# An edge-gated graph layer on one core: what GpSimd waits for between its trains of gathers

## The chip, the cores and the metric

The kernel runs on one core of a Trainium2 chip. The metric is the device time of one execution in microseconds (us). Engines are called as in the profile: PE (TensorE), DVE (VectorE), ACT (ScalarE), POOL (GpSimd), SP (SyncE).

## What is computed

A graph of 12500 nodes with 64 features and 412500 edges, sorted by target node, with 32 attributes each. Cut to what matters:

```python
h = relu(layernorm(x))                    # [12500, 64]
h0 = edge_attr @ W0 + b0                  # [412500, 64]
t = gelu(gelu(h0) @ W1 + b1) @ W2 + b2
score = (h0 + t) @ W3 + b3                # [412500, 64]
msg = h[src] * score                      # one gathered row for each edge
wV = segment_sum(msg, dst) / max(count, 1)
out = x + wV @ Wo + bo
```

## The kernel before

The edges are worked on in 403 blocks of 1024 (8 tiles of 128). For each block:

- **SP** loads the edge attributes twice (`pair`, `act_in`), four blocks ahead, and every eight blocks the source indices (`idx`).
- **POOL** issues eight indirect DMAs (L329), one for each tile: each fetches 128 rows of `h` by `src` into a slot of `rows`. There are 16 slots, one for each block of a ring of 16 (`G_RING`). Their landings count up a semaphore for each slot, `gathered[slot]`.
- **PE** does four things in this order for a step b: `second` (L437, `ps_h1`, of block b), `first` (L431, `ps_h0`, of block b + 1), `sums` (L455, `ps_w`, of block b - 1) and `last` (L446, `ps_s`, the score of block b). Each ends with one increment of a semaphore: `h1_done`, `h0_done`, `sums_done`, `score_done`.
- **ACT** takes the Gelu of `ps_h0` (L386) and of `ps_h1` (L391, two halves).
- **DVE** builds a one-hot matrix (L607), multiplies score by gathered rows into `msg` (L615, waits for `score_done` and `gathered`), and adds the window of sums into `acc` (L720, waits for `sums_done`).

`ps_s`, `ps_h1`, `ps_h0`, `ps_w` have two buffers each: names that end in a belong to even blocks, those in b to odd ones. After block 391 PE and DVE turn the finished part of `acc` into output (`project_early`, L484), and the last five blocks before it each carry a large DVE addition, L678. The gathers of the first 16 blocks are issued at the start, the first six from `x` itself before `h` is stored. Those of block b + 16 are issued in step b of POOL's loop, `gather_ahead`, after

```python
pool.wait_ge(msg_done, b + 1)                            # the slot is free again
if s % 2 == 0:
    pool.wait_ge(score_done, b + (G_RING - LAG + 1))     # LAG = 8
```

So at every second block POOL waits until PE has scored the block eight before the one whose rows it is about to gather, and then issues 16 gathers in a row.

Of the kernel before, what the change touches and what calls it, by code (L numbers as in the profile page):

```python
# [32 lines left out]
TILES = 8  # L33
# [15 lines left out]
G_RING = 16  # L49
IDX_GROUP = 8  # L50
IDX_GROUPS = 4
LAG = 8
IN_RING = 4
RAW = 6
LN_ROWS = 25
# [19 lines left out]
def edge_gated_layer(nc, x, edges, src, dst, dst_rows, weights, out):  # L75

    with ExitStack() as ctx:
# [6 lines left out]
        def sem(name):  # L84
            return ctx.enter_context(nc.semaphore(name))
# [83 lines left out]
        gathered = [sem(f"gathered{s}") for s in range(G_RING)]  # L169
# [4 lines left out]
        score_done = sem("score_done")  # L174
# [29 lines left out]
        def blocks_loop(eng, first, end, unroll, step):  # L204

            turns = (end - first) // unroll
            if turns < 2:
                turns = 0
            else:
                with eng.Fori(0, turns) as i:  # L210
                    for u in range(unroll):
                        step(i * unroll + (first + u), first + u)
            for b in range(first + turns * unroll, end):
                step(b, b)

        def uses(b, ring):

            return (b >> ring.bit_length() - 1) + 1

        def tiles_of(b):  # L220
            return LAST_TILES if isinstance(b, int) and b == NB - 1 else TILES
# [95 lines left out]
        @block.gpsimd  # L317
        def _(pool):
            pool.iota(iota_i[:, :], pattern=[[1, WIN]], base=0, channel_multiplier=0
                      ).then_inc(set_up, 1)  # L320

            def gather(b, s, table):
                slot, part, at = s % G_RING, s // IDX_GROUP % IDX_GROUPS, s % IDX_GROUP
                if at == 0:
                    pool.wait_ge(idx_in[part], uses(b, IDX_GROUP * IDX_GROUPS) * 16)

                pool.sem_inc(gathers_begun, 1)
                for t in range(tiles_of(b)):
                    pool.indirect_dma_start(  # L329
                        rows[:, slot, t, :], None, table,  # L330
                        bass.IndirectOffsetOnAxis(ap=idx[:, part, at, t:t + 1], axis=0),
                    ).then_inc(gathered[slot], 16)

            for b in range(RAW):
                gather(b, b, x)

            pool.wait_ge(h_out, 32 * LN_STEPS)
            for b in range(RAW, G_RING):
                if b == G_RING // 2:

                    pool.wait_ge(bounds_step, 1 + 2 * CHUNKS)
                    pool.sem_inc(gathers_begun, 1)
                gather(b, b, h_dram)

            def gather_ahead(b, s):

                pool.wait_ge(msg_done, b + 1)
                if s % 2 == 0:

                    pool.wait_ge(score_done, b + (G_RING - LAG + 1))  # L350
                gather(b + G_RING, s + G_RING, h_dram)

            blocks_loop(pool, 0, NB - G_RING, IDX_GROUP * IDX_GROUPS, gather_ahead)


# [490 lines left out]
```

## Time and profile before

| | |
|---|---|
| median of 3 runs | 4955.2 us (4943.95 to 4957.94) |
| the profiled execution: time | 4910.35 us |
| its span, first to last instruction | 4908.4 us |
| granted TensorE clock, mean | 0.999 of full speed (2.4 GHz) |
| busy share of the span | PE 77%, POOL 63%, ACT 20%, DVE 14% |
| gathers on POOL | 3175 of `h`, 3026.5 us busy, 953 ns each |
| DMA | 46 GB/s over the span |

A busy share is an average over the span. The profile's time of a gather on POOL is the making of its descriptors, not the arrival of its rows. "Idle before" is the time that an engine stood still before an instruction, and behind the arrow stands what ended it; "remote" stands where the profile finds no instruction of this core that ended just then, and "issue" where no wait is seen.

### The profile page before, as it was taken

The numbers are of one execution on the slowest core, as the hardware profiler recorded it, in microseconds if no ns is written. First come the engines' busy times: TensorE is split into PE (matmuls) and PEld (weight loads), VectorE is DVE, ScalarE is ACT, GpSimd is POOL, SyncE is SP. The second block draws the span as 40 slices with busy tenths as digits, with TensorE's granted clock in tenths as the row PEclk, the third lists the DMA queues.
The fourth block names the chain that finished last, engine by engine and source line by source line (L and its number), as shares of the span: only waits on it lengthen the run. The fifth ranks groups of instructions, "written<-read, shape, count | busy, mean of one in ns | idle before, by whom it ended". The sixth has DMA issues, their size and how long they took to land.

```text
span 4908.4 us, 44284 instructions
## 1 busy us (share of the span) xinstructions
PE 3760.6 (77%) x14718; PEld 2533.1 (52%) x14719; DVE 708.9 (14%) x1349; ACT 987.5 (20%) x1332; POOL 3082.5 (63%) x3228
## 2 busy tenths in 40 slices
PE   2487777777777777777777777777777777777788
PEld 1355555555555555555555555555555555555566
DVE  5011111111111111111111111111111111111122
ACT  3112112221122211221122211222112121121211
POOL 7366666666666666666666666666666666666661
PEclk9999999999999999999999999999999999999999
DMA  4111111111111111111111111111111111111111
GB/s 122 28 46 44 45 44 46 46 45 44 44 46 46 44 45 44 46 47 44 44 45 45 46 44 44 44 45 47 44 44 46 44 47 44 44 46 44 46 37 47
DMA packets 223796, 227.46 MB, mean 46 GB/s; under 512 B 118540, under 2 KB 118669, under 8 KB 223352
## 3 DMA queue, kind: packets, MB, share of 16 engines
q0 software_dynamic: 103136, 105.82, 9.9%
q1 hardware_dynamic: 119968, 117.76, 8.4%
q10 hardware_dynamic: 616, 3.20, 0.2%
q14 instruction: 68, 0.56, 0.0%
q8 instruction: 8, 0.13, 0.0%
HBM read 220.11 MB, written 6.40 MB: 46 GB/s over the span
## 4 chain that ended last, share of the span: by engine, by line
another core or an unknown queue 63%; PE 25%; DVE 4%; DVEq 3%; issue 3%; POOL 1%; ACT 0%; DMA 0%; ACTq 0%; POOLq 0%
PE ps_sb L446 14%; PE ps_wa L455 8%; DVE msg L615 3%; DVEq L715 2%; POOL rows L329 1%; DVEq L614 1%; PE ps_sa L446 1%; PE ps_h1a L437 0%; PE ps_h0a L431 0%; PE ps_h0b L431 0%; PE ps_wb L455 0%; PE ps_h1a L484 0%; PE ps_h1b L437 0%; DVE acc L720 0%
## 5 line engine op out<-in xcount | busy, mean ns | idle before, releaser
L329 POOL DMA_INDIRECT rows<-h_rows,idx x3175 | 3026.5, 953 | 1739.0 <-issue 1005.5
L455 PE MATMUL ps_wa<-ln_sq,msg 128*65 128x64 f32 x3230 | 407.2, 319 | 1035.2 <-DVE msg L615 1035.2
L455 PEld LDWEIGHTS ps_wa<-ln_sq,msg 128*65 128x65 f32 x3230 | 369.7, 229 | 1348.6 <-DVE msg L615 1335.1
L391 ACT ACTIVATE act_in<-ps_h1b,wp 64x512 f32<-64x512 f32 x402 | 275.0, 684 | 2446.5 <-remote 2377.6
L446 PE MATMUL ps_sa<-w_last,act_in 97*128 97x64 f32 x3232 | 729.9, 420 | 11.1 <-ACT act_in L391 9.2
L446 PE MATMUL ps_sb<-w_last,act_in 97*128 97x64 f32 x3216 | 728.1, 421 | 0.6 <-ACT act_in L391 0.6
L446 PEld LDWEIGHTS ps_sa<-w_last,act_in 97*128 97x128 f32 x3232 | 711.9, 332 | 13.0 <-ACT act_in L391 9.0
L446 PEld LDWEIGHTS ps_sb<-w_last,act_in 97*128 97x128 f32 x3216 | 710.4, 333 | 2.3 <-issue 1.5
L615 DVE TENSOR_TENSOR msg<-ps_sa,rows 128x512 f32<-128x512 f32 x202 | 139.7, 691 | 3034.6 <-remote 2973.3
L391 ACT ACTIVATE act_in<-ps_h1a,wp 64x512 f32<-64x512 f32 x404 | 276.4, 684 | 1308.7 <-PE ps_h1a L437 1019.2
L455 PEld LDWEIGHTS ps_wb<-ln_sq,msg 128*65 128x65 f32 x3216 | 368.1, 229 | 303.5 <-issue 302.9
L437 PE MATMUL ps_h1b<-g,wp 128*128 128x512 f32 x402 | 406.4, 1112 | 35.7 <-ACT g L386 29.9
L431 PE MATMUL ps_h0a<-pair,wp 64*128 64x512 f32 x404 | 418.5, 1137 | 1.9 <-issue 1.9
L437 PE MATMUL ps_h1a<-g,wp 128*128 128x512 f32 x404 | 408.3, 1114 | 15.1 <-ACT g L386 13.4
L431 PE MATMUL ps_h0b<-pair,wp 64*128 64x512 f32 x402 | 416.5, 1138 | 0.0
L455 PE MATMUL ps_wb<-ln_sq,msg 128*65 128x64 f32 x3216 | 405.6, 319 | 1.5 <-issue 1.5
L615 DVE TENSOR_TENSOR msg<-ps_sb,rows 128x512 f32<-128x512 f32 x201 | 139.0, 692 | 985.9 <-PE ps_sb L446 905.8
L607 DVE TENSOR_TENSOR ln_sq<-dst_i,iota 128x512 f32<-128x512 f32 x403 | 277.8, 690 | 8.4 <-issue 8.4
L431 PEld LDWEIGHTS ps_h0a<-pair,wp 64*128 64x128 f32 x404 | 101.2, 309 | 304.3 <-issue 304.2
L431 PEld LDWEIGHTS ps_h0b<-pair,wp 64*128 64x128 f32 x402 | 100.3, 310 | 302.4 <-issue 302.4
L386 ACT ACTIVATE g<-ps_h0b,wp 128x512 f32<-128x512 f32 x201 | 138.2, 687 | 89.9 <-PE ps_h0b L431 51.5
L386 ACT ACTIVATE g<-ps_h0a,wp 128x512 f32<-128x512 f32 x202 | 138.9, 688 | 12.4 <-PE ps_h0a L431 5.5
(63 smaller groups left out, 719.4 us busy)
## 6 DMA issues: line engine op xcount, KB each, us to landing
pair<-in_edges SPq DMA_DIRECT2D x403, 128.0 KB
act_in<-in_edges SPq DMA_DIRECT2D x403, 128.0 KB
rows<-h_rows,idx POOLq DMA_INDIRECT x3175
xs<-in_x SPq DMA_DIRECT2D x4, 700.0 KB
h_rows<-ln_d ACTq DMA_DIRECT2D x4, 700.0 KB
dst_i<-in_dst SPq DMA_DIRECT2D x1, 1612.0 KB
idx<-in_src SPq DMA_DIRECT2D x50, 32.0 KB
rows<-in_dst_rows SPq DMA_DIRECT2D x4, 384.0 KB
```

Source lines behind the costliest of these rows:

```text
L329: pool.indirect_dma_start(rows[:, slot, t, :], None, table, bass.IndirectOffsetOnAxis(ap=idx[:, part, at, t:t + 1], axis=0),).then_inc(gat ...
L386: act.activation(g1[:, s % 2, :], ps_h0[s % 2][:, :], ACT.Gelu, bias=b0).then_inc(g1_done, 1)
L391: act.activation(act_in[0:D, s % IN_RING, g, :], ps_h1[s % 2][g * D:(g + 1) * D, :], ACT.Gelu, bias=wp[g * D:(g + 1) * D, C_B1:C_B1 + 1]). ...
L431: pe.matmul(ps_h0[s % 2][:, :], w0, pair[:, s % IN_RING, :], start=True, stop=True).then_inc(h0_done, 1)
L437: pe.matmul(ps_h1[s % 2][:, :], w1, g1[:, s % 2, :], start=True, stop=True).then_inc(h1_done, 1)
L446: mm = pe.matmul(ps_s[s % 2][:, t * D:(t + 1) * D], act_in[:, s % IN_RING, g, j * P:(j + 1) * P], w_last[:, :], start=(t == 0), stop=(t == ...
L455: last = pe.matmul(window, msg[:, s % 2, t, :], onehot[:, t, :], start=(t == 0), stop=(t == n - 1))
L607: return dve.tensor_tensor(to, rel.unsqueeze(2).to_broadcast([P, TILES, WIN]), iota_tiles, ALU.is_equal)
L614: dve.wait_ge(gathered[s % G_RING], (uses(b, G_RING) - 1) * 16 * TILES + 16 * n)
L615: dve.tensor_tensor(msg[:, s % 2, 0:n, 0:D], ps_s[s % 2][:, 0:n * D].rearrange("p (t d) -> p t d", d=D), rows[:, s % G_RING, 0:n, :], ALU. ...
L715: base = dve.value_load(base_b[0:1, one(b)], min_val=0, max_val=N - 1)
```

## The change

In place of the score of eight blocks back, POOL waits at every second block for the landing of all gathers of the block before. The wait now stands in `gather` itself, so it also holds in the first 16 blocks; the wait for the free slot stays.

```diff
-LAG = 8
@@ def gather(b, s, table):
                 if at == 0:
                     pool.wait_ge(idx_in[part], uses(b, IDX_GROUP * IDX_GROUPS) * 16)
+                if s > 0 and s % 2 == 0:
+
+                    pool.wait_ge(gathered[(s - 1) % G_RING], uses(b - 1, G_RING) * 16 * TILES)
 
                 pool.sem_inc(gathers_begun, 1)
@@ def gather_ahead(b, s):
                 pool.wait_ge(msg_done, b + 1)
-                if s % 2 == 0:
-
-                    pool.wait_ge(score_done, b + (G_RING - LAG + 1))
                 gather(b + G_RING, s + G_RING, h_dram)
```

`uses(b, ring)` is b // ring + 1, the number of times that the slot has been used with block b.

## Rows read from the trace of the kernel before

**Rows 1.** The page: the chain that ended last, its shares by engine.

```profile
another core or an unknown queue 63%; PE 25%; DVE 4%; DVEq 3%; issue 3%; POOL 1%; ACT 0%; DMA 0%; ACTq 0%; POOLq 0%
```

**Rows 2.** Timeline, one train of gathers and its ends: start, duration, engine, instruction, idle before.

```profile
2001.15 2.02 PE L437 MATMUL ps_h1b<-g,wp 128*128 128x512 f32 x2
...
2005.52 0.94 POOL L329 DMA_INDIRECT rows<-h_rows,idx  x1 [0.30 <-issue]
...
2009.49 1.39 ACT L391 ACTIVATE act_in<-ps_h1b,wp 64x512 f32<-64x512 f32 x2 [12.78 <-remote]
2009.62 0.69 DVE L615 TENSOR_TENSOR msg<-ps_sa,rows 128x512 f32<-128x512 f32 x1 [13.98 <-remote]
...
2010.20 0.94 POOL L329 DMA_INDIRECT rows<-h_rows,idx  x1 [3.73 <-remote]
...
2010.37 2.02 PE L455 MATMUL ps_wa<-ln_sq,msg 128*65 128x64 f32 x16 [5.20 <-DVE msg L615]
...
2016.01 0.69 DVE L615 TENSOR_TENSOR msg<-ps_sb,rows 128x512 f32<-128x512 f32 x1 [4.64 <-PE ps_sb L446]
...
2028.95 0.95 POOL L329 DMA_INDIRECT rows<-h_rows,idx  x1 [0.30 <-issue]
```

**Rows 3.** Waits of the stretch 241 to 4698: who waited for whom, us, times, longest.

```profile
PE ps_wa L455 <- DVE msg L615: 960.2, 187, 5.7
...
POOL rows L329 <- remote: 666.5, 176, 4.1
```

**Rows 4.** Busy time by stretch: us, then PE, PEld, DVE, ACT, POOL, clock, DMA.

```profile
187.00:241.00 54.00, 52.09 (x213) 36.61 (x214) 9.40 (x19) 14.90 (x20) 0.00 (x0) 1.00 0.11 30
241.00:1241.00 1000.00, 786.59 (x3064) 525.71 (x3062) 130.82 (x258) 202.07 (x277) 645.22 (x680) 1.00 0.18 45
```

**Rows 5.** Groups by line, stretch 241 to 4698: the gathers.

```profile
L329 POOL DMA_INDIRECT rows<-h_rows,idx x3024 | 2872.0, 950 | 1644.2 <-issue 914.9 <-remote 666.5 <-PE ps_sa L446 62.8
```

**Rows 6.** Timeline of the start, blocks 1 to 8.

```profile
95.51 0.69 DVE L615 TENSOR_TENSOR msg<-ps_sb,rows 128x512 f32<-128x512 f32 x1 [3.67 <-remote]
...
107.55 1.39 ACT L391 ACTIVATE act_in<-ps_h1a,wp 64x512 f32<-64x512 f32 x2 [17.77 <-remote]
...
177.72 0.95 POOL L329 DMA_INDIRECT rows<-h_rows,idx  x1 [0.30 <-issue]
...
187.54 0.69 DVE L615 TENSOR_TENSOR msg<-ps_sa,rows 128x512 f32<-128x512 f32 x1 [82.23 <-remote]
...
240.72 0.69 DVE L615 TENSOR_TENSOR msg<-ps_sa,rows 128x512 f32<-128x512 f32 x1 [7.43 <-PE ps_sa L446]
...
241.45 0.95 POOL L329 DMA_INDIRECT rows<-h_rows,idx  x1 [62.78 <-PE ps_sa L446]
```

**Rows 7.** Timeline: the last gather of block 5, and DVE, which waits for its landing.

```profile
73.07 0.95 POOL L329 DMA_INDIRECT rows<-in_x,idx  x1 [0.30 <-issue]
...
75.46 1.22 DVE L580 TENSOR_REDUCE ln_sum<-rows 128x16 f32<-128x1024 f32 x1 [12.80 <-DMA rows<-in_x,idx]
```

**Rows 8.** Timeline of POOL, DVE and ACT in blocks 387 to 391, with L678.

```profile
4715.96 0.94 POOL L329 DMA_INDIRECT rows<-h_rows,idx  x1 [0.31 <-remote]
4717.21 2.80 POOL L329 DMA_INDIRECT rows<-h_rows,idx  x1 [0.30 <-issue]
...
4717.10 1.48 DVE L678 TENSOR_TENSOR xs<-xs,wp 120x1280 f32<-120x1280 f32 x1
...
4719.34 0.69 ACT L386 ACTIVATE g<-ps_h0a,wp 128x512 f32<-128x512 f32 x1 [2.12 <-remote]
...
4731.63 0.69 DVE L615 TENSOR_TENSOR msg<-ps_sa,rows 128x512 f32<-128x512 f32 x1 [5.52 <-PE ps_sa L446]
...
4740.81 0.69 DVE L615 TENSOR_TENSOR msg<-ps_sb,rows 128x512 f32<-128x512 f32 x1 [6.15 <-PE ps_sb L446]
```

**Rows 9.** Timeline: two scored blocks after the last gather.

```profile
4854.85 0.69 DVE L615 TENSOR_TENSOR msg<-ps_sb,rows 128x512 f32<-128x512 f32 x1 [7.55 <-PE ps_sb L446]
...
4864.03 0.69 DVE L615 TENSOR_TENSOR msg<-ps_sa,rows 128x512 f32<-128x512 f32 x1 [7.54 <-PE ps_sa L446]
```

## The prediction, on record before the changed kernel ran

> **What bounds the kernel now.** I read the page first. Its chain of what ended last gives 63% of the span to no instruction at all and only 25% to PE [rows 1], so the span is mostly a wait whose author the profile can't name. The timeline of one stretch shows the wait. PE ends the matmuls of ps_h1b at 2001.15 + 2.02 = 2003.17, yet ACT, which waits for nothing else, starts on them at 2009.49; DVE starts on ps_sa, finished before them, at 2009.62 [rows 2]. Both are released within 0.13 us of each other by "remote". PE's work was done; its signals came 6.3 us late. PE itself then waits 5.20 us for DVE's msg [rows 2], and this happens once for two blocks, 187 times, 960 us between 241 and 4698 [rows 3].
>
> When are the signals late? The reader should look at POOL beside them. In 187 to 241 POOL is idle and PE is busy 52.09 of 54 us; from 241 on POOL is busy 645 of 1000 us and PE 787 [rows 4]. After the last gather a block takes 4864.03 - 4854.85 = 9.18 us [rows 9]. In a train of 16 gathers, 2010.20 to 2028.95 + 0.95 = 2029.90 [rows 2], the signals of the first ten us come in time (msg of ps_sb at 2016.01) and those due later wait for the end of the train: 2009.49 is 3.03 us after the previous train's last gather (2005.52 + 0.94 = 2006.46) [rows 2]. At the start, where POOL issues gathers without a break until 178.67, blocks 1 and 2 are 187.54 - 95.51 = 92 us apart [rows 6]. So a long unbroken train of gathers holds back PE's signals, and a pause sets them free. I don't know the mechanism, only this law.
>
> The cycle before is therefore: a train of 19.70 us, then a pause that lasts until the held score arrives, since it is just this score that POOL waits for, 3.73 us [rows 2]; POOL's waits of this kind are 666.5 / 176 = 3.79 us [rows 3]. 19.70 + 3.79 = 23.5 us for two blocks. Checked against the whole: from block 8 (240.72) to block 391 (4740.81) it is 4500.1 / 383 = 11.75 us a block [rows 6, 8], 3024 / 16 = 189 trains [rows 5].
>
> **The change part by part.** *Removed:* the wait for the score. POOL's pause no longer depends on when PE's signals get through. *Added:* a wait for the landing of the previous block's last gather. Its price has one near row: the last gather of block 5 ends on POOL at 74.02, and DVE, which waited for its landing, starts at 75.46, 1.44 us later [rows 7]. POOL's own way from a released wait to its next gather is 2010.20 - 2009.49 = 0.71 us [rows 2]. Together a pause of 2.15 us in place of 3.79. The bounds: not below 1.7 (DVE's own start taken out of the 1.44 and the reaction overlapped), not above 2.6 (landing beside full traffic). I take 2.15. The cycle becomes 19.70 + 2.15 = 21.85 us, 10.93 a block.
>
> What is queued behind this wait on POOL is only the next gathers and their index wait. Who waits for them is DVE's msg, and the gathers run seven to eight blocks ahead, some 80 us, so nobody feels it directly. SP's index loads hang on msg_done, which freed them for four groups of eight blocks ahead; POOL reaches at most two groups ahead, so they stay in time. The wait for the free slot stays: POOL may now run up to 16 blocks ahead, but if PE does two blocks for each train it never gets there.
>
> Does PE do two blocks in 21.85 us? It needs 18.4 [rows 9]. If the held signals come 3.03 us after a train's last gather as now, that is 0.9 us after the new train's start; the next score, 6.5 us on (2016.01 after 2009.49, [rows 2]), lies at 7.4 us in the train, still in its free part; the one after at about 16.5 us, held until the next pause. Two scores a cycle, then, and POOL is the bound.
>
> The open question is whether a pause of 2.15 us frees them at all, because POOL resumes before the 3.03 us are over. The rows nearest to it are those of blocks 387 to 391. There DVE's long addition (1.48 us) stretches single gathers: that at 4717.21 takes 2.80 in place of 0.95, so POOL makes no headway for 1.85 us [rows 8]. ps_h0a, held until then, reaches ACT at 4719.34, 2.4 us after the previous gather's end at 4716.90, while POOL has not been given a longer break [rows 8]. With such an addition at every block and no real pause, msg follows msg after 4740.81 - 4731.63 = 9.18 us, PE's full speed [rows 8, 9]. A break of 1.85 us in the train thus does what the long one does. But these breaks come once a block, those of the change once in two blocks, after 20 us of gathers; that is why I am not sure.
>
> The page "GPSIMD Engine Reference" of the Trainium skill (section Specifications) says that POOL shares its interface to SBUF with DVE and contends with DVE instructions that have two SBUF inputs; by it these stretches are POOL at rest, not POOL at other work, and the trace agrees (2.80 us beside the two-input addition of 1.48 us). The page "DMA: Bandwidth & Descriptors" puts the fixed cost of a DMA at about 2.0 us, mostly the receipt of the write; as an estimate from it, a landing wait of 1.05 us behind the descriptors, a pause of 1.8 and a total some 65 us lower. No gather's landing is timed by itself in the rows, so I stay with the 2.15.
>
> **The sum**, against the profiled execution's 4910.35 us:
>
> - Blocks 8 to 391: 383 x (11.75 - 10.93) = -314 us.
> - Start, blocks 1 to 8: now 240.72 - 95.51 = 145 us, most of it the 82 us in which the signals were held [rows 6]. The new wait also breaks the trains there, at blocks 8, 10, 12 and 14, so 7 x 10.93 = 77 us: -68. Bounds 0 (the signals stay held as now) and -75; I take -60, for the first blocks' uneven start.
> - Early projection (project_early) and the last eleven blocks: POOL is still some seven blocks ahead and is done during the projection; unchanged, 0.
>
> Together 4910 - 314 - 60 = 4536 us. The median of the runs lies 45 us above the profiled execution (4955.2 against 4910.35); I carry this over: 4580 us, -7.6%. With the pause between 1.7 and 2.6 us and the start's bounds: 4490 to 4650.
>
> **The rivals.**
>
> 1. *The short pause frees nothing* (slower). The signals need 3 us of silence, POOL is back after 2.15. Then POOL runs on to the 16th slot and stops there for msg_done. For it: at the start signals were held for 82 us, and the first came 8.9 us after the last gather (187.54 against 178.67) [rows 6], so a deep jam isn't gone at once. Against it: rows 8. Its time: release 3.03 us after the train, msg 0.13 + 0.69, POOL 0.71, a pause of 4.6 us; 24.3 a cycle, +0.8 x 192 = +155, and +40 at the start, where PE no longer gets its free run of 187 to 241: about 5150 us, up to 5400 if a landing wait falls amid each train as well. Chance 0.20.
> 2. *Some pauses work, some don't.* Each miss costs PE about one cycle of 21.85 us that it can't regain while POOL stays two blocks a cycle. The gain of 374 us is used up by 17 misses among 192 trains; with 4 to 15 misses the time is 4650 to 4930. For it: the start of the present kernel, where single signals slip through at odd moments (107.55) [rows 6]. Chance 0.12.
> 3. *No change*, within 0.3%: POOL is faster and PE takes it up with waits elsewhere, or misses happen to balance: 4955. No row speaks for it; chance 0.04.
>
> My forecast has the remaining 0.64. The point that decides between it and rival 1 is one number: whether PE's signals arrive within about 3 us of a train's end although POOL restarts at 2.15.
>
> **Numbers.** 0.3% is about what a measurement here can tell from no change. Faster: 0.64 + 0.11 = 0.75; same 0.04; slower 0.21. The range reaches from 4480 over the partly working pauses and no change to 4990, which leaves out nearly only rival 1; the forecast's own range is 4490 to 4650.
>
> **What the changed profile would show.** If right: trains of 16 gathers with 2.1 to 2.2 us before every 17th; ACT and DVE released "remote" about 3 us after a train's last gather, with POOL already in its next; PE's wait before ps_w about 3.5 us in place of 5.2; no gap of 80 us at the start and none of 62.78 us on POOL; two blocks in 21.9 us. If rival 1 holds: POOL's pauses of 4 to 5 us ended just after DVE's msg, and a lead of 16 blocks. Rival 2 would show as PE waits of 20 us and more. The prediction fails if the pause is much longer than 2.6 us, or if the score due 7.4 us into a train is already held (then PE would do one block a train and rival 1 takes over).

## The result, and the profile after

The changed kernel takes 5181.21 us (median of 4 runs, 5179.42 to 5183.77), the kernel before 4955.07 us beside it: ratio 1.0469, 95% interval 1.0446 to 1.0491. It is 4.7% slower; the forecast was 7.6% faster. The profiled execution took 5179.42 us. Its page:

```profile
span 5177.4 us, 44320 instructions
...
PE 3753.1 (72%) x14718; PEld 2528.3 (49%) x14719; DVE 709.0 (14%) x1349; ACT 986.1 (19%) x1332; POOL 3096.5 (60%) x3228
...
PEclk9555555555555555555555555555555555555555
...
L331 POOL DMA_INDIRECT rows<-h_rows,idx x3175 | 3042.0, 958 | 1864.6 <-issue 1154.5
```

No engine has noticeably more work than before: the gathers are 3042.0 us in place of 3026.5, PE has 3753.1 in place of 3760.6, and no share is higher. Nearly all of the added time is waiting. The granted clock is 0.5 (1.2 GHz) from the second slice on, where before it was 2.4 GHz; that looks like a cause and isn't one (below). Line numbers have moved by one or two: POOL L331, DVE's msg L614, ACT L385 and L390, PE L430 to L454.

The waits of the changed kernel (who waited for whom, us in total, times, longest):

```profile
DVE msg L614 <- remote: 3293.0, 193, 83.1
...
PE ps_wa L454 <- DVE msg L614: 1210.9, 191, 8.9
...
POOL rows L331 <- DVE msg L614: 705.6, 144, 6.6
```

These sums are over the whole span. The second line has 191 waits and 1035.2 us in the trace before: PE now waits longer. The third is new: POOL waited for the held score itself [rows 3], and waits now for DVE's msg, which comes after it. The landing is not what ends its pauses. The timeline of one cycle (start, duration, idle before):

```profile
2001.57 0.94 POOL L331 DMA_INDIRECT rows<-h_rows,idx  x1 [0.30 <-issue]
...
2005.40 1.39 ACT L390 ACTIVATE act_in<-ps_h1b,wp 64x512 f32<-64x512 f32 x2 [14.02 <-remote]
2005.55 0.69 DVE L614 TENSOR_TENSOR msg<-ps_sa,rows 128x512 f32<-128x512 f32 x1 [16.33 <-remote]
...
2007.15 0.98 POOL L331 DMA_INDIRECT rows<-h_rows,idx  x1 [4.64 <-DVE msg L614]
...
2030.30 0.69 DVE L614 TENSOR_TENSOR msg<-ps_sa,rows 128x512 f32<-128x512 f32 x1 [16.61 <-remote]
...
2031.90 0.97 POOL L331 DMA_INDIRECT rows<-h_rows,idx  x1 [4.93 <-DVE msg L614]
```

The last gather ends at 2001.57 + 0.94 = 2002.51, the held signals reach ACT 2.89 us and DVE 3.04 us later, DVE multiplies for 0.69, and POOL is back 0.91 us after that: 4.64 us. Before, POOL was back 0.71 us after the score, beside DVE's multiplication [rows 2]. The cycle is now 2031.90 - 2007.15 = 24.75 us.

How did POOL come to be 16 blocks ahead? The start shows it:

```profile
135.12 0.94 POOL L331 DMA_INDIRECT rows<-h_rows,idx  x1 [2.35 <-issue]
136.10 0.69 DVE L614 TENSOR_TENSOR msg<-ps_sa,rows 128x512 f32<-128x512 f32 x1 [19.21 <-remote]
...
179.10 0.94 POOL L331 DMA_INDIRECT rows<-h_rows,idx  x1 [2.29 <-DMA rows<-h_rows,idx]
...
181.27 0.69 DVE L614 TENSOR_TENSOR msg<-ps_sb,rows 128x512 f32<-128x512 f32 x1 [43.41 <-remote]
...
201.13 0.94 POOL L331 DMA_INDIRECT rows<-h_rows,idx  x1 [2.30 <-issue]
...
223.13 0.94 POOL L331 DMA_INDIRECT rows<-h_rows,idx  x1 [2.33 <-issue]
...
245.00 0.94 POOL L331 DMA_INDIRECT rows<-h_rows,idx  x1 [2.22 <-DMA rows<-h_rows,idx]
...
266.13 0.69 DVE L614 TENSOR_TENSOR msg<-ps_sa,rows 128x512 f32<-128x512 f32 x1 [83.10 <-remote]
...
284.00 1.09 POOL L331 DMA_INDIRECT rows<-h_rows,idx  x1 [6.57 <-DVE msg L614]
290.12 0.69 DVE L614 TENSOR_TENSOR msg<-ps_sa,rows 128x512 f32<-128x512 f32 x1 [5.84 <-PE ps_sa L445]
```

Here the pauses are near the predicted ones, 2.22 to 2.35 us for a landing. Two of the six are followed soon by a held msg (136.10 and 181.27, 0.98 and 2.17 us after POOL is back); four are not (157.14, 201.13, 223.13, 245.00), and the last three of these fall into 83 us without a msg. At 284.00 the ring is full, since POOL has issued the gathers of blocks 0 to 22 and needs block 7's msg for the next, and the first pause ended by msg comes.

The 269.0 us between the spans (5177.4 - 4908.4) are then accounted for. Block 8 is reached at 290.12 in place of 240.72 [rows 6]: +49.4. From block 8 to 391, at 5020.81 in the trace after, it takes 4730.7 us in place of 4500.1: +230.6, or 12.35 us a block against 11.75. The rest is 156.6 against 167.6 us: -11.0. The medians lie only 226 us apart, because the profiled execution before was 45 us below the median of its kernel and the one after only 2 us below.

### The profile page after: what moved, and what is told of

Same layout as the page of the kernel before. It is cut to its first block, busy times and chain, and to the rows that moved or that the text cites. A ratio compares the mean times of both kernels' runs of the same rounds, so it can differ in the third digit from the quotient of the medians.

```text
span 5177.4 us, 44320 instructions
## 1 busy us (share of the span) xinstructions
PE 3753.1 (72%) x14718; PEld 2528.3 (49%) x14719; DVE 709.0 (14%) x1349; ACT 986.1 (19%) x1332; POOL 3096.5 (60%) x3228
## 4 chain that ended last, share of the span: by engine, by line
another core or an unknown queue 65%; PE 24%; DVE 4%; DVEq 3%; issue 2%; ACT 0%; POOL 0%; DMA 0%; ACTq 0%
PE ps_sb L445 13%; PE ps_wa L454 8%; DVE msg L614 3%; DVEq L714 2%; DVEq L613 1%; PE ps_sa L445 1%; PE ps_h1a L483 0%; PE ps_h1b L483 0%; PE ps_h1a L436 0%; PE ps_h0a L430 0%; PE ps_wb L454 0%; DVE acc L719 0%; PE ps_h1b L436 0%; PE ps_h0b L430 0%
## 5 line engine op out<-in xcount | busy, mean ns | idle before, releaser
L331 POOL DMA_INDIRECT rows<-h_rows,idx x3175 | 3042.0, 958 | 1864.6 <-issue 1154.5
L454 PE MATMUL ps_wa<-ln_sq,msg 128*65 128x64 f32 x3230 | 406.8, 319 | 1277.0 <-DVE msg L614 1210.9
L454 PEld LDWEIGHTS ps_wa<-ln_sq,msg 128*65 128x65 f32 x3230 | 369.4, 228 | 1590.3 <-DVE msg L614 1509.9
L390 ACT ACTIVATE act_in<-ps_h1b,wp 64x512 f32<-64x512 f32 x402 | 274.5, 683 | 2729.8 <-remote 2673.4
L614 DVE TENSOR_TENSOR msg<-ps_sa,rows 128x512 f32<-128x512 f32 x202 | 139.7, 692 | 3300.0 <-remote 3234.9
L454 PEld LDWEIGHTS ps_wb<-ln_sq,msg 128*65 128x65 f32 x3216 | 367.7, 228 | 334.0 <-issue 333.5
L390 ACT ACTIVATE act_in<-ps_h1a,wp 64x512 f32<-64x512 f32 x404 | 275.7, 683 | 1308.0 <-issue 994.4
L454 PE MATMUL ps_wb<-ln_sq,msg 128*65 128x64 f32 x3216 | 405.1, 319 | 32.8 <-issue 32.8
L430 PE MATMUL ps_h0a<-pair,wp 64*128 64x512 f32 x404 | 417.5, 1135 | 2.9 <-issue 2.9
L430 PE MATMUL ps_h0b<-pair,wp 64*128 64x512 f32 x402 | 415.3, 1135 | 1.1 <-issue 1.1
L614 DVE TENSOR_TENSOR msg<-ps_sb,rows 128x512 f32<-128x512 f32 x201 | 139.1, 692 | 996.3 <-PE ps_sb L445 933.6
L430 PEld LDWEIGHTS ps_h0a<-pair,wp 64*128 64x128 f32 x404 | 100.7, 309 | 304.6 <-issue 304.5
L430 PEld LDWEIGHTS ps_h0b<-pair,wp 64*128 64x128 f32 x402 | 100.2, 309 | 302.8 <-issue 302.8
L385 ACT ACTIVATE g<-ps_h0b,wp 128x512 f32<-128x512 f32 x201 | 138.1, 687 | 65.5 <-PE ps_h0b L430 31.3
L385 ACT ACTIVATE g<-ps_h0a,wp 128x512 f32<-128x512 f32 x202 | 138.8, 687 | 15.3 <-remote 5.0
```

The source lines that it names most:

```text
L331: pool.indirect_dma_start(rows[:, slot, t, :], None, table, bass.IndirectOffsetOnAxis(ap=idx[:, part, at, t:t + 1], axis=0),).then_inc(gat ...
L385: act.activation(g1[:, s % 2, :], ps_h0[s % 2][:, :], ACT.Gelu, bias=b0).then_inc(g1_done, 1)
L390: act.activation(act_in[0:D, s % IN_RING, g, :], ps_h1[s % 2][g * D:(g + 1) * D, :], ACT.Gelu, bias=wp[g * D:(g + 1) * D, C_B1:C_B1 + 1]). ...
L430: pe.matmul(ps_h0[s % 2][:, :], w0, pair[:, s % IN_RING, :], start=True, stop=True).then_inc(h0_done, 1)
L454: last = pe.matmul(window, msg[:, s % 2, t, :], onehot[:, t, :], start=(t == 0), stop=(t == n - 1))
L614: dve.tensor_tensor(msg[:, s % 2, 0:n, 0:D], ps_s[s % 2][:, 0:n * D].rearrange("p (t d) -> p t d", d=D), rows[:, s % G_RING, 0:n, :], ALU. ...
```

## The experiments

The kernel before is itself found at two levels here. In some sets its median is 4902 to 4955 us, as above; in others 4215 to 4219 us, and the traces of those sets show no signal late. I didn't find what decides. By the numbers on record it isn't the chip alone: the first set, which was free, and the third, which was held, were both run on the chip numbered 7. I call the sets *held* and *free*; each ratio compares kernels of one set. The expectations of the first set were written for a held one.

The rate of the gathers is the measure used throughout. "Cycle" is 4270 us (330 to 4600 of the trace) by the number of gathers in it, times 16; in free sets 3670 us (330 to 4000). The profiled execution of the kernel before is the one of 4910.35 us. The groups by line show these numbers, here for the changed kernel and for g3 (count | busy, ns of one | idle before):

```profile
L331 POOL DMA_INDIRECT rows<-h_rows,idx x2757 | 2636.7, 956 | 1633.7 <-issue 1001.3 <-DVE msg L614 632.5
```

```profile
L334 POOL DMA_INDIRECT rows<-h_rows,idx x2902 | 2773.1, 956 | 1497.9 <-issue 1497.9
```

| kernel | set | gathers | cycle, us | time, us | ratio to the kernel before |
|---|---|---|---|---|---|
| before | held | 2898 | 23.58 | 4955.07 | 1 |
| changed | held | 2757 | 24.78 | 5181.21 | 1.0469 [1.0446, 1.0491] |
| f1_changed | held | 2774 | 24.63 | 5150.84 | 1.0511 [1.0487, 1.0534] |
| f2_no_wait | held | 2806 | 24.35 | 5097.28 | 1.0398 [1.0376, 1.0421] |
| f4_rest_block | held | 2806 | 24.35 | 5085.37 | 1.0374 [1.0350, 1.0399] |
| g2_idle6 | held | 2738 | 24.95 | 5208.87 | 1.0622 [1.0601, 1.0642] |
| f3_idle12 | held | 2888 | 23.66 | 4963.90 | 1.0101 [1.0034, 1.0168] |
| g3_idle16 | held | 2902 | 23.54 | 4844.74 | 0.9891 [0.9864, 0.9918] |
| g1_both | held | 2877 | 23.75 | 4914.78 | 1.0017 [1.0007, 1.0028] |
| g4_start | held | 2901 | 23.55 | 4877.50 | 0.9947 [0.9927, 0.9966] |
| e1_no_wait | free | 2854 | 20.57 | 4214.79 | 1.0000 [0.9990, 1.0009] |
| h4_changed | free | 2637 | 22.27 | 4549.51 | 1.0786 [1.0765, 1.0807] |
| e2_idle12 | free | 2522 | 23.28 | 4750.80 | 1.1270 [1.1252, 1.1289] |
| e3_every_block | free | 2459 | 23.88 | 4870.54 | 1.1557 [1.1538, 1.1576] |
| e4_rest_block | free | 2713 | 21.64 | 4424.75 | 1.0499 [1.0481, 1.0516] |

The theory after the result was A: held signals come free only after nearly 3 us without a gather; the landing pause is too short for it, and with the score's wait gone POOL runs ahead until the full ring stops it, where it restarts a msg later than before. The expectations name it and its rivals by letters.

### First set: no wait, longer pauses, more pauses (free)

e1 and f2 are the changed kernel without its new wait:

```diff
-                if s > 0 and s % 2 == 0:
-
-                    pool.wait_ge(gathered[(s - 1) % G_RING], uses(b - 1, G_RING) * 16 * TILES)
```

e2 and f3 lengthen the pause by 12 increments of an unused semaphore, g2 by 6, g3 by 16:

```diff
                     pool.wait_ge(gathered[(s - 1) % G_RING], uses(b - 1, G_RING) * 16 * TILES)
+                    for _ in range(12):
+                        pool.sem_inc(idle, 1)
```

e3 waits for the landing at every block (`if s > 0:`). e4 and f4 have no landing wait; a memset of POOL, 128 x 1024 f32, whose result is unused, stands before the gathers of every block:

```diff
+                if s > 1 and s % 1 == 0:
+                    pool.wait_ge(rested, b - 1)
                 pool.sem_inc(gathers_begun, 1)
+                if s > 0 and s % 1 == 0:
+                    pool.memset(rest[:, :], 0.0).then_inc(rested, 1)
```

> Neither wait: POOL waits only for the free slot (msg_done). Theory A (the held signals come free only some 3 us after the last gather, and the landing wait of the changed kernel is already over when POOL gets its slot, so it costs nothing): the same time as the changed kernel, 5150 to 5210 us, trains of 16 ended by DVE's msg, 24.7 us for two blocks. Theory L (the landing wait is what costs): faster than the changed kernel by up to 2 us a train, 4800 to 4960 us.

> The changed kernel, and after each landing wait 12 increments of an unused semaphore on POOL's sequencer, about 0.1 us each, so that the pause between two trains is about 3.4 us in place of 2.3. Theory A (3 us of silence free the signals): the signals get through in each pause, POOL is the bound at 19.8 + 3.4 = 23.2 us for two blocks, 4780 to 4900 us. Theory C (the changed kernel is slower because TensorE's granted clock is 0.51 in it): the pause changes nothing while the clock is low, 5180 us or more. If the pause must be longer still, the time stays at 5180 too, with the clock at either level.

> The landing wait at every block: trains of 8 gathers (9.7 us) with pauses of 2.3 us. Theory A (a pause of 2.3 us frees nothing, whatever the train): held signals as in the changed kernel, 5180 us or more. Theory J (the jam builds up with the length of the train, and trains under 10 us never hold a signal for long, as in blocks 387 to 391 of the kernel before): POOL is the bound at 24.0 us for two blocks, 4900 to 5000 us, no remote wait over 3 us.

> No landing wait; in its place POOL clears 1024 elements of an unused tile at every block from block 1 on, about 1 us in which it makes no descriptors, like the stretched gathers of blocks 387 to 391 of the kernel before. Theory J: two blocks in about 22.2 us, 4560 to 4750 us. Theory A: signals held, 5180 us or more.

Measured: e1 4214.79 us, e2 4750.80, e3 4870.54, e4 4424.75, the kernel before 4214.60. The levels were missed by far, because the set was free. The timeline of e1:

```profile
2002.70 1.39 ACT L387 ACTIVATE act_in<-ps_h1b,wp 64x512 f32<-64x512 f32 x2 [6.90 <-PE ps_h1b L433]
...
2004.91 0.69 DVE L611 TENSOR_TENSOR msg<-ps_sa,rows 128x512 f32<-128x512 f32 x1 [8.49 <-DMA rows<-h_rows,idx]
```

ACT is released by PE and not by "remote", and DVE waits for its rows: the gathers are the bound, 20.57 us for 16, without any break. Then every pause costs something: e3 has two of 2.26 us for 16 gathers and lies 3.31 us a cycle above e1, e2 has one of 3.27 and lies 2.71 above. That is a little less than their length, because 0.30 us stand between two gathers in any case and the gathers are shorter beside pauses (944 and 966 ns against 982). So this set says nothing on A, but two things of use. The removed wait alone changes nothing where no signal is held (ratio 1.0000). And the clock makes no difference to this kernel: the profiled run of e1 was granted 0.999 and took 4215.80 us, its nine others 0.519 and 4213.16 to 4217.12 us.

### Second set: the same, in a held set

> The changed kernel once more, beside the kernel before on one chip. The first experiments ran on a chip on which the kernel before took 4215 us and no signal of TensorE came late. Theory H (whether the signals are held is a property of the chip): on such a chip POOL is the bound, 21.95 us for two blocks, 4570 to 4620 us, 8 to 10% slower than before; on a chip that holds signals 5180 us against 4955. The granted clock, 0.52 or 1.0, makes no difference either way.

> Neither wait, on the same chip. If the chip holds signals: theory A 5150 to 5210 us, as the changed kernel, since both wait for the 16th slot; theory L under 4960 us. If it holds none: 4215 us, as before.

> The changed kernel with pauses of about 3.2 us. If the chip holds signals: theory A 4750 to 4900 us, faster than the kernel before there; if 3.2 us don't free them, 5180 us or more. If it holds none: 4751 us again.

> A rest of about 0.85 us on POOL at every block. If the chip holds signals: theory J 4425 to 4750 us, theory A 5180 us or more. If it holds none: 4425 us again.

The kernel before took 4901.70 us, f1 5150.84: the result repeats. **f2**, without any wait, took 5097.28. Most of the loss, 196 of 249 us, is therefore there without the added wait; it comes with the removed one. The timeline of f2 shows POOL stopped by the ring, 4.44 us each time:

```profile
2002.59 1.39 ACT L387 ACTIVATE act_in<-ps_h1a,wp 64x512 f32<-64x512 f32 x2 [13.56 <-remote]
2002.72 0.69 DVE L611 TENSOR_TENSOR msg<-ps_sb,rows 128x512 f32<-128x512 f32 x1 [16.27 <-remote]
...
2004.19 1.10 POOL L328 DMA_INDIRECT rows<-h_rows,idx  x1 [4.44 <-DVE msg L611]
```

Against the trace before, f2 loses 38.0 us up to block 8 (278.76) and 157.8 us from there to block 391 (4936.68). The landing wait adds the other 54 us, 0.28 us a cycle. Of f2's three runs one was granted 0.999 and two about 0.51, at 5096.79 to 5097.41 us: in a held set, too, the clock doesn't make the loss. The changed kernel itself was never seen at the upper level.

**f3**, with a pause of about 3.2 us, took 4963.90: the signals get through, mostly. **f4** took 5085.37 at a clock of 0.999. Its rests (2018.18 to 2019.32, 1.14 us) come once a block, a shape near to that of the additions of blocks 387 to 391, and yet signals are held and the ring stops POOL:

```profile
2018.17 0.98 POOL L333 MEMSET rest<- 128x1024 f32 x1
2019.32 0.95 POOL L335 DMA_INDIRECT rows<-h_rows,idx  x1 [0.17 <-issue]
...
2042.89 0.69 DVE L618 TENSOR_TENSOR msg<-ps_sa,rows 128x512 f32<-128x512 f32 x1 [14.73 <-remote]
2044.23 0.95 POOL L333 MEMSET rest<- 128x1024 f32 x1 [4.41 <-DVE msg L618]
```

That speaks against short trains with short rests as the remedy, though weakly: such a rest is 0.84 us longer than the usual 0.30 between two gathers, where the additions of blocks 387 to 391 lengthen a gather by 1.0 to 1.9 us. Two of its three runs were at 0.999 and one at 0.512, 5081.72 to 5089.18 us, which speaks once more against the clock.

Theory A doesn't come out of this set whole. It wanted the same time for f2 as for the changed kernel (5150 to 5210 us), 4750 to 4900 for f3 and at least 5180 for f4; all three missed, by 53, 64 and 95 us. The part that failed in f2 is that the landing wait costs nothing once the ring is full.

### Third set: how long must the pause be, and is the score's wait what is missed (held)

g2 and g3 have 6 and 16 increments. g1 keeps the landing wait and puts the score's wait back:

```diff
                 pool.wait_ge(msg_done, b + 1)
+                if s % 2 == 0:
+
+                    pool.wait_ge(score_done, b + (G_RING - LAG + 1))
                 gather(b + G_RING, s + G_RING, h_dram)
```

g4 is the kernel before with the landing wait and 12 increments in the first 16 blocks alone (`if 0 < s < G_RING and s % 2 == 0:`).

> The changed kernel with the score wait put back beside the landing wait. On a chip that holds signals (before 4900 to 4955): theory A says that the loss comes from what was removed, not from what was added: POOL starts again 0.7 us after the held score and no longer 0.7 us after the msg made from it, pauses 3.8 to 4.1 us, and the time is within 1% of the kernel before, 4880 to 4990. Theory L (the landing wait itself costs): 5150. On a chip that holds none (before 4215): POOL-bound, 4590 to 4620, as the changed kernel would be.

> The changed kernel with 6 increments after each landing wait, pauses of about 2.75 us: between the 2.3 that freed nothing and the 3.2 that freed the signals 2.6 to 3.0 us after the last gather. If what counts is that POOL is silent until then: signals held past the pause, ring full, 5100 to 5180 us where signals are held. If they only need the landing and a little time: 4850 to 4970. On a chip that holds none: about 4690.

> 16 increments, pauses of about 3.5 us, fixed and not tied to the score. With 12 (3.2 us) the signals came free in each pause, but PE fell behind now and then and POOL met the full ring (mean pause 3.7). If the small rest of margin was the reason: mean pause 3.6, 4840 to 4900 us where signals are held, faster than the kernel before; if not, 4930 to 4990 as with 12. On a chip that holds none: about 4810.

> The kernel before, and in its first 16 blocks alone the landing wait with 12 increments at every second block. If pauses of 3.2 us keep the signals moving at the start too, where the kernel before stands for some 80 us: 30 to 60 us faster than before where signals are held; where none are held, 10 to 25 us slower than before.

The kernel before took 4903.84 us. **g1** took 4914.78, ratio 1.0017: with the score's wait back, the loss is gone although the landing wait stays. That is A's second half, shown by itself. Its steady part:

```profile
2017.50 1.39 ACT L394 ACTIVATE act_in<-ps_h1b,wp 64x512 f32<-64x512 f32 x2 [12.29 <-remote]
2017.63 0.69 DVE L618 TENSOR_TENSOR msg<-ps_sa,rows 128x512 f32<-128x512 f32 x1 [15.49 <-remote]
2018.52 0.95 POOL L332 DMA_INDIRECT rows<-h_rows,idx  x1 [4.25 <-DVE msg L618]
```

The profile names msg here, but POOL is back 0.20 us after msg's end, and 0.08 in the middle one of 180 such pauses, where in the changed kernel it is never back before 0.91. By these times it was the score that released it, not the msg. The landing wait still has a price in g1: from block 8 (212.55) to block 391 (4745.19) it takes 32.5 us longer than the kernel before, and gains 28.2 in the start.

**g2** took 5208.87, more than the changed kernel and than expected. Its start, with pauses that are mostly 2.65 to 2.84 us:

```profile
204.40 0.95 POOL L334 DMA_INDIRECT rows<-h_rows,idx  x1 [2.69 <-issue]
...
210.41 0.69 DVE L617 TENSOR_TENSOR msg<-ps_sa,rows 128x512 f32<-128x512 f32 x1 [19.52 <-remote]
...
226.96 0.95 POOL L334 DMA_INDIRECT rows<-h_rows,idx  x1 [2.72 <-issue]
...
230.95 0.69 DVE L617 TENSOR_TENSOR msg<-ps_sb,rows 128x512 f32<-128x512 f32 x1 [18.79 <-remote]
```

One msg for a train of 16 gathers, 6.0 and 4.0 us after POOL has resumed (up to 10 in the rest of the start): PE does one block where POOL does two, so the ring fills all the same, and then the six increments come on top of the full ring's wait (pauses of 5.17 to 5.22 us near 2013 and 2038).

**g3**, with pauses of mostly 3.5 to 3.7 us, took 4844.74. Its start:

```profile
163.30 0.69 DVE L617 TENSOR_TENSOR msg<-ps_sb,rows 128x512 f32<-128x512 f32 x1 [15.44 <-remote]
...
163.69 0.94 POOL L334 DMA_INDIRECT rows<-h_rows,idx  x1 [3.72 <-issue]
...
170.97 0.69 DVE L617 TENSOR_TENSOR msg<-ps_sa,rows 128x512 f32<-128x512 f32 x1 [5.93 <-PE ps_sa L448]
...
187.12 0.95 POOL L334 DMA_INDIRECT rows<-h_rows,idx  x1 [3.57 <-issue]
```

Each held msg starts just before POOL resumes, two a cycle. In the steady part it is no faster than the kernel before (23.54 against 23.58 us). Its gain is the start: block 8 at 170.97 in place of 240.72 [rows 6], 69.8 us earlier, and block 391 at 4672.01 in place of 4740.81 [rows 8], 68.8 us earlier. So the profiled traces put all of it there.

**f3** between them is marginal. In its start most pauses of about 3.2 us end just after the msg (msg 139.19, POOL 139.23), and two fail, with POOL back at 185.66 and 301.43 and the msg 0.82 and 1.53 us later. The second of them:

```profile
301.43 0.94 POOL L334 DMA_INDIRECT rows<-h_rows,idx  x1 [3.20 <-issue]
302.96 0.69 DVE L617 TENSOR_TENSOR msg<-ps_sb,rows 128x512 f32<-128x512 f32 x1 [11.78 <-remote]
...
324.27 0.69 DVE L617 TENSOR_TENSOR msg<-ps_sa,rows 128x512 f32<-128x512 f32 x1 [19.56 <-remote]
324.28 0.94 POOL L334 DMA_INDIRECT rows<-h_rows,idx  x1 [3.19 <-issue]
```

**g4** took 4877.50, 26 us less than the kernel before, where 30 to 60 were expected. Its first pauses work, the one that ends at 186.10 misses the msg by 0.80 us, and then the unbroken gathers of the next blocks hold the signals again:

```profile
186.10 0.94 POOL L335 DMA_INDIRECT rows<-h_rows,idx  x1 [3.16 <-issue]
...
253.79 0.69 DVE L621 TENSOR_TENSOR msg<-ps_sb,rows 128x512 f32<-128x512 f32 x1 [55.71 <-remote]
```

### Fourth and fifth set: does the addition of DVE free the signals? (free)

What misled the forecast were the blocks with DVE's long addition [rows 8]. These kernels give every block from the start an addition like it, 120 x 1280 f32, on unused data: h1 to the changed kernel, h2 and i1 to the one before, h3 and i2 to the one without either wait. h4 is the changed kernel as it is.

```diff
                 message(b, s)
+                if s > EARLY_BLOCKS - 10:
+                    return
+                if s > 1:
+                    dve.wait_ge(widened, b - 1)
+                dve.tensor_tensor(pad_out, pad_in0, pad_in1, ALU.add).then_inc(widened, 1)
```

> The changed kernel, and in every block up to 385 an addition of 120 x 1280 elements on DVE with two inputs in SBUF (1.48 us, its result is not used), as the kernel has it in blocks 387 to 391. Theory S (the stretch of a gather beside this addition frees the signals, more than a plain pause of its length): no late scores, POOL-bound at 22 + 2 x 1.1 to 2 x 1.9 us for two blocks, 4750 to 5050 us where the kernel before takes 4900. Theory A (only some 2.9 us of silence frees them): late scores as before, 5200 us or more.

> The kernel before with the same addition in every block. Theory S: no late scores, and with them POOL's wait for the score falls away: 20 us of gathers and 2.2 to 3.8 us of stretch for two blocks, 4650 to 4900 us. Theory A: the stretches come on top of held signals, 4950 to 5200 us.

> The same addition with neither wait, as in blocks 387 to 391 where POOL met no wait either. Theory S: 4650 to 4900 us, no late scores. Theory A: 5100 us or more, as with neither wait and no addition (5097).

> The changed kernel beside these. Where signals are held: 1.045 to 1.055 times the kernel before. Where none are (before 4215): 4590 to 4620 us, 9% slower, bound by POOL at 21.95 us for two blocks.

> Where signals are held (before 4900 to 4955): theory S 4360 to 4900 us, no late scores; theory A 4950 to 5200 us. Where none are: 4367 us again.

> Where signals are held: theory S 4360 to 4900 us, no late scores; theory A 5100 us or more. Where none are: 4363 us again.

Both sets came out free, the kernel before at 4218.48 and 4218.69 us. h1 took 4847.11 us (1.1492 [1.1469, 1.1514]), h2 4367.32 (1.0345 [1.0325, 1.0365]), h3 4362.72 (1.0336 [1.0314, 1.0358]), i1 4366.21 (1.0341 [1.0321, 1.0361]), i2 4365.60 (1.0339 [1.0315, 1.0363]). The additions stretch the gathers: 1029 ns each in h2 against 982 in e1, which takes the time of the kernel before, and 1062 in h1 against 965 in h4. Times 3175 gathers that is 149 and 308 us, which is what the additions cost on top of the kernel before (149 us) and, nearly, of the changed one (298). But no signal was held, so none could be freed; the question stays open. In h2, h3, i1 and i2 the one run at the upper clock was 10 to 14 us shorter than those at 0.517 or 0.518: here the clock is worth about 0.3%.

h4 is a miss in a small way (4549.51 us against 4590 to 4620). It is also the one clean view of the landing pause in the steady part:

```profile
2002.90 0.94 POOL L331 DMA_INDIRECT rows<-h_rows,idx  x1 [0.30 <-issue]
2005.33 0.69 DVE L614 TENSOR_TENSOR msg<-ps_sb,rows 128x512 f32<-128x512 f32 x1 [8.54 <-DMA rows<-h_rows,idx]
...
2006.08 0.94 POOL L331 DMA_INDIRECT rows<-h_rows,idx  x1 [2.23 <-DMA rows<-h_rows,idx]
```

The landing reaches DVE 1.49 us after the gather's end at 2003.84, and POOL resumes after 2.23 us. The change is slower in a free set too, by 7.9%: a cycle of 22.27 us against 20.57 in e1, the price of a pause where gathers are the bound.

## Why the prediction was wrong

**The bound** was read rightly for a held set. There trains of gathers hold PE's signals, and a pause frees them: g1, g3 and f2 move the time by POOL's waits alone, with the same work on every engine. As a law it was too wide, since in a free set e1 issues its gathers without any break and no signal is late.

**The price of the landing wait** was right: 2.15 us predicted, 2.22 to 2.35 measured at the start, 2.23 in the pause shown of h4, within the bounds of 1.7 and 2.6. The page "DMA: Bandwidth & Descriptors" of the Trainium skill (section "Anatomy of one DMA — SWDGE (gpsimd) path") gives a DMA a fixed cost of about 2.0 us, from which the prediction estimated 1.8. In h4 it is 0.94 + 1.49 = 2.43 us from the gather's start to DVE's, so the trace decides for the longer pause.

**The step that failed** is the one that the prediction called the open question, whether "a pause of 2.15 us frees them at all". It was answered by "A break of 1.85 us in the train thus does what the long one does", from the additions in blocks 387 to 391 [rows 8]. As a length of pause that is refuted: 2.3 us frees a signal now and then (after two of six pauses in the start of the changed kernel, and then none for 83 us), 2.7 us lets one signal through a train and late, 3.2 us mostly works, 3.6 us always did in the start of g3. The stretched gathers did more than a bare pause of their length in the kernel before, and again in g3, which was held too:

```profile
4644.47 0.69 DVE L617 TENSOR_TENSOR msg<-ps_sa,rows 128x512 f32<-128x512 f32 x1 [3.19 <-PE ps_sa L448]
...
4646.16 2.53 POOL L334 DMA_INDIRECT rows<-h_rows,idx  x1 [0.31 <-issue]
...
4653.65 0.69 DVE L617 TENSOR_TENSOR msg<-ps_sb,rows 128x512 f32<-128x512 f32 x1 [5.78 <-PE ps_sb L448]
...
4662.83 0.69 DVE L617 TENSOR_TENSOR msg<-ps_sa,rows 128x512 f32<-128x512 f32 x1 [6.14 <-PE ps_sa L448]
```

They don't do it each time: in g4 a gather of 1.83 us at 4672.12 was followed by a held msg, 17.48 us after the one before. The changed kernel can't tell, because its last gather ends at 4989.20, before the blocks in question. What the stretch does stays open, since the kernels made for it met no held signals.

**The forecast cycle** of 21.85 us fell with that step (24.78 measured), and so did the start: the forecast had -60 us, and it was +49.4. The start term was right for a pause that is long enough: g3 gains 69.8 us there (bounds 0 and 75). That PE does two blocks in 21.85 us with held signals was never seen; the 22.27 us of h4 are a cycle without any. Three smaller terms: the end was put at 0 and gave -11.0 us, because POOL's lead of 16 blocks lets it finish before the projection; the 45 us carried over from profiled run to median were 2 in the changed kernel; and the forecast's own range didn't follow from its bounds, since a pause of 2.6 us and a start of 0 add up to about 4725 us and not to 4650.

**Rival 1** came true, by its own steps: release to ACT 2.89 us after the train (3.03), msg, POOL's reaction 0.91 (0.71), a pause of 4.64 (4.6), a cycle of 24.75 (24.3), the start +49.4 (+40), 5181 us (about 5150). It had a chance of 0.20. What spoke for it, POOL back at 2.15 us against signals at 3.03 us and a jam of 82 us at the start, were rows of the very case in question; what spoke against it was a row of another case, in which DVE was at work as well. The first should have weighed more.

**Rival 2** is what f3 is, and g2 and the changed kernel in their starts: pauses that free some signals. **The removed wait**, which the forecast counted only as a gain, was also what let POOL resume 0.7 us after the score. Without it POOL runs on to the full ring and resumes after the msg; that is 196 of the 249 us (f2), and g1 gives it back.

**The best version where signals are held** is g3, 1.1% faster than the kernel before; the same kind of pause (e2) costs 12.7% in a free set. No kernel tried is known to be faster in both kinds, and g3 and g4 weren't run in a free one.

## What to carry to other kernels

Ask of every wait in a producer's loop what else it does: this one looked like a bound on how far POOL runs ahead, and it was also the pause, of just the needed length, in which held signals came through. A change from a wait that adapts (until the held signal is here) to one that doesn't (until a landing) must be measured against the length that is needed, and evidence from a stretch with another engine at work isn't evidence for a bare pause. Take the price of a pause from a kernel in which nothing is held as well, since there it costs time and frees nothing (1.70 us a cycle for the pause of 2.2 us in h4).

## What the runs showed of the hardware

- In the held sets, PE's signals that fall due late in a train of indirect DMAs are held. In the kernel before, the score used 5.8 us into the train that starts at 2010.20 came in time, and the next, whose matmuls end 14.8 us into it, didn't. In the steady part the held ones mostly arrive 2.8 to 3.5 us after its last gather (3.0 to 3.5 in the changed kernel, 2.8 to 3.4 in f2, 3.0 to 3.9 in g2), whatever POOL waits for. How it comes about wasn't found.
- The same kernel has two times on this hardware, 4215 to 4219 us and 4902 to 4955 us (medians), steady within a set. In the faster one no signal is held, though e1 has no break between its gathers. What decides wasn't found.
- The granted clock changed little: 0.519 or 0.999 at 4213 to 4217 us in e1, 0.51 or 0.999 at 5097 us in f2, 0.512 or 0.999 at 5082 to 5089 us in f4; in h2, h3, i1 and i2 the run at the upper level was 10 to 14 us shorter than those at 0.517 or 0.518.
- A two-input addition of DVE (1.48 us) lengthens a gather that meets it: 1.99 to 2.87 us in place of 0.95 in blocks 387 to 391 of the kernel before.
- An increment of a semaphore on POOL prolongs its pause by about 0.08 us: (3.6 - 2.3) / 16.
